# Squares of keys and queries: moved from GpSimd to VectorE, taken out of the projection's PSUM bank, and summed four tiles at a time

## The chip, the cores and the metric

The kernel runs on one core of a Trainium2 chip. The metric is the device time of one execution, in microseconds (us). The core has TensorE (PE in the rows, its weight loads PEld), VectorE (DVE), ScalarE (ACT), GpSimd (POOL) and SyncE (SP), each of which runs its own instructions in order and waits for the others by semaphores.

## The reference

One transformer block in fp32, on x of shape (2, 2048, 256): attention with 16 heads of 64, a residual and a layer norm, a gated feed-forward part with two hidden layers of 1024, another residual and layer norm. What the change touches is the RMS norm of keys and queries at the head of attention:

```python
def _rmsnorm(x, w):
    var = jnp.mean(jnp.square(x), axis=-1, keepdims=True)
    return x * jax.lax.rsqrt(var + EPS_RMS) * w

q = (x @ Wq).reshape(B, T, H, D)
k = (x @ Wk).reshape(B, T, H, D)
v = (x @ Wv).reshape(B, T, H, D)
q = _rmsnorm(q, q_rms_w)
k = _rmsnorm(k, k_rms_w)
gate_logits = jnp.einsum('bthd,hd->bht', k, u_n) / math.sqrt(D)
gate = jax.nn.softplus(gate_logits)
bias = -dist[None, None] * omega_eff[None, :, None, None] * gate[:, :, None, :]
scores = jnp.einsum('bihd,bjhd->bhij', q, k) * scale + bias
attn = jax.nn.softmax(scores, axis=-1)
y = jnp.einsum('bhij,bjhd->bihd', attn, v).reshape(B, T, H * D)
```

The mean of squares is over the 64 values of a head, for each token, head, and for q and k.

## The kernel before, in words

Three parts follow one another: attention (until about 2170 us), ffn_up and ffn_down. The change is in attention alone.

Attention works through 16 pairs of heads. One list of steps, made by `attention_steps` (line 80), sets the order on every engine: each engine walks the same list and issues what is its own, so a step's place in the list is its place in every queue. The scores of the current heads drive the list; the preparation of the next pair (projection, squares, sums, roots, norms, gate, transposes "turn", row maxima "max") is woven in at times written out by hand, in units of a head's work, t0 being the start of the pair's first head.

For pair p, 16 steps `project` (p, t), one for each 128 tokens, multiply x by the pair's weights: six matmuls of 386 columns (line 883) into one of two PSUM banks that such work takes in turn, `ps_p` and `ps_t` (`work_bank`, line 336). The 386 columns are k and q of both heads (4 x 64), two gate logits and v of both heads. ScalarE copies the bank into tile t of `raw` in SBUF (line 591) and counts up `pj_free`; `work_free` (line 339) makes TensorE wait for that count before it writes the same bank two work steps later.

GpSimd squares k and q of half the tiles (8 x 64 = 512 elements a partition) in one instruction, `square` (line 541): eight a pair, into a ring of four in `sq`. VectorE reduces each over the 64 values, `sum` (line 730): eight a pair, into `sumsq`. Then VectorE makes the inverse root by Newton steps (`root`, line 731 on; first instruction line 746), the gate (line 754 on) and the eight norms (line 766).

VectorE also has the row maxima: `max` steps, 40 a head. TensorE multiplies q by k into one of two banks `ps_m` (line 907) and VectorE takes the maximum (line 814, or 811 on the diagonal) and counts up `mx_free`; TensorE's matmul of max m waits for VectorE's max m-2:

```python
if m >= 2:
    pe.wait_ge(mx_free, m - 1)
```

TensorE's order is thus: project, max, scores, values and the rest of values of the current head, all in one queue; a wait at a max holds all that stands behind it.

Before the first pair, the VectorE step `weights` of pair 0 copies the gate's weights (line 717) and then runs `constants(4)` (line 720), a chain of constants that ends with the memset of `c_all` (line 697); the steps of pair 0 stand behind it in VectorE's queue. GpSimd's first square waits for its end (`s_const`). `sq` doubles as room for constants (`mask_f`, `pos`, `rms_in`) before the first squares.

GpSimd's main work is `e_lo`, the rest of the exponentials' split in two numbers (line 385).

Of the kernel before, what the change touches and what calls it, by code (L numbers as in the profile page):

```python
# [12 lines left out]
H, D = 16, 64  # L13
# [66 lines left out]
def attention_steps():  # L80
# [4 lines left out]
    def at(when, *step):  # L85
        extra.append((when, len(extra), step))
# [7 lines left out]
    for p in range(PAIRS):  # L94
# [5 lines left out]
        for i in range(4):  # L100
            at(t0 - 1.44 + 0.05 * i, "square", p, i)
            at(t0 - 1.38 + 0.05 * i, "sum", p, i)
            at(t0 - 1.22 + 0.04 * i, "square", p, i + 4)
            at(t0 - 1.16 + 0.04 * i, "sum", p, i + 4)
# [72 lines left out]
def attention(nc, x, wq, wk, wv, q_rms_w, k_rms_w, omega, u, yt_dram, recip_dram, rows_dram):  # L177
    ctx = ExitStack()
    with ctx:
# [20 lines left out]
        sq = sb("sq", [P, 4, HT, D])  # L200
# [38 lines left out]
        rms_in = sq[:, 1, 0:1, :]  # L239
        mask_f = sq[:, 0, 0:2, :].rearrange("p a d -> p (a d)")  # L240
        pos = sq[:, 2:4, :, :].rearrange("p i a d -> p (i a d)")
# [28 lines left out]
        pj_full = sem("pj_full")  # L270
        pj_free = sem("pj_free")
        sq_done = sem("sq_done")
# [205 lines left out]
        def _(gp):  # L478
# [42 lines left out]
            for step in steps:  # L521
# [11 lines left out]
                if step[0] == "square":  # L533
                    p, i = step[1:]
                    col, rows = (q_cols(0), q_cols(1), k_cols(0), k_cols(1))[i % 4], slice(i // 4 * HT, (i // 4 + 1) * HT)
                    gp.wait_ge(pj_free, TT * p + HT * (i // 4 + 1))
                    if p == 0 and i == 0:
                        gp.wait_ge(s_const, 1)
                    if p or i >= 4:
                        gp.wait_ge(ss_done, 8 * p + i - 3)  # L540
                    nc.gpsimd.tensor_tensor(sq[:, i % 4, :, :], raw[:, rows, col:col + D], raw[:, rows, col:col + D], ALU.mult).then_inc(sq_done, 1)
# [23 lines left out]
        def _(act):  # L565
# [6 lines left out]
            for step in steps:  # L572
# [9 lines left out]
                if step[0] == "project":  # L582
# [8 lines left out]
                    nc.scalar.activation(raw[:, t, :], work_bank(step)[:, 0:WCOLS], ACT.Copy).then_inc(pj_free, 1)  # L591
# [38 lines left out]
        def _(dve):  # L630
# [70 lines left out]
            for step in steps:  # L701
# [24 lines left out]

                if step[0] == "sum":
                    p, i = step[1:]
                    dve.wait_ge(sq_done, 8 * p + i + 1)
                    nc.vector.tensor_reduce(sumsq[:, i % 4, i // 4 * HT:(i // 4 + 1) * HT], sq[:, i % 4, :, :], AX.X, ALU.add).then_inc(ss_done, 1)  # L730
                if step[0] == "root":
                    p, i = step[1:]
                    rs, root_t, _, _ = pair_scratch(p)
                    if i == 0:
                        rooted = [ROOT * p]
                        dve.wait_ge(ss_done, 8 * (p + 1))
                        work_free(dve, step)
# [955 lines left out]
```

## Time and profile before

| | |
|---|---|
| median of 3 runs | 3400.02 us (3398.07 to 3406.59) |
| the profiled execution's own time | 3401.34 us |
| its span, from the first to the last instruction | 3399.6 us |
| mean granted TensorE clock | 0.970 |
| busy: TensorE | 3158.8 us (93%) |
| busy: ScalarE | 1794.1 us (53%) |
| busy: VectorE | 1659.2 us (49%) |
| busy: GpSimd | 1499.9 us (44%) |
| squares on GpSimd (line 541) | 128 instructions |
| sums on VectorE (line 730) | 128 instructions |

Busy time is what an engine's instructions took. Matmuls overlap, so the busy time of one is longer than its distance to the next: two starts, not a duration, tell what a matmul costs. A VectorE instruction's record also overlaps the next one's by somewhat under 0.1 us. "idle before <-releaser" names the engine, tile and line whose semaphore ended an engine's idle time. The granted clock is a share of 2.4 GHz.

### The profile page before, as it was taken

Reading aid. Unit: us, or ns where it says so; the run is one execution under the profiler, and the core shown is the slowest. Engines: PE = TensorE matmul, PEld = TensorE weight load, DVE = VectorE, ACT = ScalarE, POOL = GpSimd, SP = SyncE. Lnnn points to the kernel's source line nnn. Section 1 sums busy time; section 2 is a strip of 40 time slices with the busy share of each in tenths; the row PEclk is TensorE's granted clock in tenths of the full one; section 3 lists DMA queues with packets and bytes.
Section 4 is the critical chain, followed back from the end, with each engine's and each line's share of the span. In section 5 each row is a group of like instructions: output and inputs, shape, how many; then the busy total and the mean of one; then the engine's idle time right before and its main releaser. Section 6 shows DMA issues by size and latency. Waiting matters only on the chain. (4 is left out here: it accounts for less than half of the span.)

```text
span 3399.6 us, 45979 instructions
## 1 busy us (share of the span) xinstructions
PE 3158.8 (93%) x15472; PEld 2456.8 (72%) x15472; DVE 1659.2 (49%) x3920; ACT 1794.1 (53%) x3057; POOL 1499.9 (44%) x1318
## 2 busy tenths in 40 slices
PE   3999999999999999999999999679999999899998
PEld 3667767767767677677677677467777778688887
DVE  6565565566565665655665666142222222232322
ACT  1576676667666766766776777532222222222222
POOL 4476676566666666666766766421111110000000
PEclk6899999999999999999999999889999999899999
DMA  2242332322432422422323323432232221312120
GB/s 76 65 92 49 73 85 46 84 68 50 95 77 61 99 61 51 100 48 67 87 46 81 76 50 85 111 110 87 87 87 87 87 87 38 107 66 75 42 71 19
DMA packets 196539, 249.12 MB, mean 73 GB/s; under 512 B 67280, under 2 KB 95056, under 8 KB 196176
## 3 DMA queue, kind: packets, MB, share of 16 engines
q1 hardware_dynamic: 196304, 246.19, 28.2%
q8 instruction: 123, 2.02, 0.3%
q14 instruction: 112, 0.92, 0.1%
HBM read 84.86 MB, written 43.52 MB: 38 GB/s over the span
## 5 line engine op out<-in xcount | busy, mean ns | idle before, releaser
L385 POOL TENSOR_TENSOR e_lo<-e_all,e_hi 128x512 fp32r<-128x512 f32 (+1 forms) x832 | 1032.1, 1249 | 654.6 <-ACT e_all L627 588.8
L627 ACT ACTIVATE e_all<-ps_s,bias 128x512 f32<-128x512 f32 (+3 forms) x1280 | 788.6, 623 | 168.3 <-PE ps_s L929 80.3
L814 DVE TENSOR_REDUCE maxes<-ps_m 128x1 f32<-128x512 f32 x768 | 521.2, 686 | 371.6 <-PE ps_m L907 368.8
L620 ACT ACTIVATE e_hi<-ps_s,bias 128x512 fp32r<-128x512 f32 (+1 forms) x832 | 560.1, 673 | 228.7 <-PE ps_s L927 134.1
L907 PE MATMUL ps_m<-k_ext,q_max 128*128 128x512 f32 (+3 forms) x1280 | 462.2, 382 | 54.3 <-DVE maxes L814 25.1
L926 PE MATMUL ps_s<-q_twice,k_split 128*128 128x512 f32 (+3 forms) x1280 | 478.0, 373 | 28.3 <-ACT e_all L627 23.3
L927 PE MATMUL ps_s<-q_ext,k_ext 128*128 128x512 f32 (+3 forms) x1280 | 469.9, 367 | 0.0
L960 PE MATMUL ps_v<-e_lo,v_main 128*66 128x512 f32 (+1 forms) x832 | 431.7, 519 | 17.3 <-POOL e_lo L385 17.3
L907 PEld LDWEIGHTS ps_m<-k_ext,q_max 128*128 128x128 f32 x1280 | 245.5, 192 | 202.5 <-DVE maxes L814 59.0
L811 DVE CUSTOM_DVE_ANT_0 ps_m<-ps_m,mask_row 128x128 f32<-128x128 f32 (+3 forms) x512 | 252.5, 496 | 282.3 <-PE ps_m L907 281.9
L949 PE MATMUL ps_v<-e_hi,v_main 128*66 128x512 f32 (+1 forms) x832 | 322.2, 387 | 0.0
L944 PE MATMUL ps_v<-e_all,v_full 128*66 128x512 f32 (+2 forms) x896 | 322.2, 441 | 0.0
L951 PE MATMUL ps_v<-e_hi,v_rest 128*66 128x512 f32 (+1 forms) x832 | 320.8, 386 | 0.0
L926 PEld LDWEIGHTS ps_s<-q_twice,k_split 128*128 128x128 f32 x1280 | 242.9, 190 | 95.8 <-issue 41.0
L1162 POOL TENSOR_TENSOR y_in<-y_in,r_in 128x512 f32<-128x512 f32 x64 | 84.2, 1317 | 450.7 <-DMA r_in<-recip_sums 450.6
L927 PEld LDWEIGHTS ps_s<-q_ext,k_ext 128*128 128x128 f32 x1280 | 243.1, 190 | 31.9
L1507 POOL TENSOR_TENSOR dn_rs<-dn_rs,dn_power 128x4 f32<-128x4 f32 x8 | 8.1, 1008 | 471.8 <-DVE dn_rs L1598 471.8
L1538 ACT ACTIVATE dn_gelu<-dn_h,dn_scale 128x512 f32<-128x512 f32 x64 | 44.0, 688 | 322.8 <-PE dn_h L1637 322.8
L1225 ACT ACTIVATE gelu<-up_h,up_scale 128x512 f32<-128x512 f32 x64 | 44.1, 689 | 309.8 <-PE up_h L1382 309.8
L1637 PE MATMUL dn_h<-a_hi,h_hi 128*128 128x512 f32 x512 | 204.0, 398 | 3.7 <-DVE a_lo L1569 3.7
L960 PEld LDWEIGHTS ps_v<-e_lo,v_main 128*66 128x66 f32 x832 | 114.8, 138 | 125.7 <-issue 45.5
L1382 PE MATMUL up_h<-p_hi,h_hi 128*128 128x512 f32 x512 | 203.7, 398 | 0.0
(247 smaller groups left out, 6112.3 us busy)
## 6 DMA issues: line engine op xcount, KB each, us to landing
q_twice<-q_max SPq DMA_DIRECT2D x256, 128.0 KB, 2.3
yt<-y_out SPq DMA_DIRECT2D x128, 130.0 KB
k_ext<-kq_hi SPq DMA_DIRECT2D x128, 128.0 KB, 2.3
q_max<-kq_hi SPq DMA_DIRECT2D x128, 128.0 KB, 2.4
k_split<-kq_hi SPq DMA_DIRECT2D x128, 128.0 KB, 2.4
k_split<-kq_lo SPq DMA_DIRECT2D x128, 128.0 KB, 2.4
q_ext<-kq_lo SPq DMA_DIRECT2D x128, 128.0 KB, 2.4
y_in<-yt SPq DMA_DIRECT2D x128, 128.0 KB, 3.1
```

Source lines behind the costliest of these rows:

```text
L385: on.tensor_tensor(e_lo[:, i % LO_RING, off:QB], e_all[:, u_ % E_RING, off:QB], e_hi[:, i % HI_RING, off:QB].bitcast(F32), ALU.subtract).t ...
L620: nc.scalar.activation(e_hi[:, i % HI_RING, off:QB], ps_s[u_ % 2][:, off:QB], ACT.Exp, bias=by).then_inc(hi_done, 1)
L627: nc.scalar.activation(e_all[:, u_ % E_RING, off:QB], ps_s[u_ % 2][:, off:QB], ACT.Exp, bias=by).then_inc(ex_done, 1)
L811: nc.vector.tensor_tensor_reduce(ps_m[m % 2][:, 0:width], ps_m[m % 2][:, 0:width], mask_row[:, QB - width:QB], 1.0, NEG, ALU.add, ALU.max, ...
L814: nc.vector.tensor_reduce(maxes[:, qt, kc:kc + 1], ps_m[m % 2][:, 0:width], AX.X, ALU.max).then_inc(mx_free, 1)
L907: nc.tensor.matmul(ps_m[m % 2][:, 0:width], q_max[s][:, qt * P:(qt + 1) * P], k_ext[s][:, kc * QB:kc * QB + width], start=True, stop=True) ...
L926: nc.tensor.matmul(out, k_split[s][:, k], q_twice[grp % Q_RING][:, off:QB], start=True, stop=False)
L927: last = nc.tensor.matmul(out, k_ext[s][:, k], q_ext[s][:, q], start=False, stop=not diag)
L944: nc.tensor.matmul(bank[0:VCOLS, off:QB], v_full[s][:, kt // TQ, kt % TQ - TQ // 2, :], e_all[:, u_ % E_RING, off:QB], start=False, stop=k ...
L949: nc.tensor.matmul(bank[0:VCOLS, off:QB], v_main[s][:, kt, :], e_hi[:, i % HI_RING, off:QB], start=kt == 0, stop=False, skip_group_check=True)
L951: nc.tensor.matmul(bank[0:VCOLS, off:QB], v_rest[s][:, kt, :], e_hi[:, i % HI_RING, off:QB], start=False, stop=False, skip_group_check=Tru ...
L960: nc.tensor.matmul(ps_v[(n * NQB + qb) % 2][0:VCOLS, off:QB], v_main[s][:, kt, :], e_lo[:, i % LO_RING, off:QB], start=False, stop=kt - TQ ...
```

## The change

For each tile of the projection, VectorE now waits for ScalarE's copy (new semaphore `pj_raw`) and multiplies the 256 columns of k and q still in the PSUM bank with the copy in `raw`; the product goes to `sq`, now a ring of eight tiles of 256. Only the end of this product counts up `pj_free` and so frees the bank (and lets GpSimd take the values). After each four tiles (in the list, just behind the `project` step of the tile after them, or in the last case behind that of the last tile), one reduction over 4 x 256 elements gives the sums of four tiles. GpSimd's eight squares and VectorE's eight sums over 512 elements are gone. `sumsq` keeps its shape, its four columns now in the order of the projection's columns.

```diff
--- before.py
+++ after.py
@@ -97,11 +97,8 @@
         at(t0 - 2.05, "weights", p)
         for t in range(TT):
             at(t0 - 1.72 + 0.030 * t, "project", p, t)
-        for i in range(4):
-            at(t0 - 1.44 + 0.05 * i, "square", p, i)
-            at(t0 - 1.38 + 0.05 * i, "sum", p, i)
-            at(t0 - 1.22 + 0.04 * i, "square", p, i + 4)
-            at(t0 - 1.16 + 0.04 * i, "sum", p, i + 4)
+        for i in range(TT // TQ):
+            at(t0 - 1.72 + 0.030 * (TQ * i + 3) + 0.03, "sum", p, i)
         for i in range(ROOT_PARTS):
             at(t0 - 1.00 + 0.01 * i, "root", p, i)
         at(t0 - 0.95, "gate a", p)
@@ -197,7 +194,7 @@
         w_lo = sb("w_lo", [P, KC, WCOLS], F32R)
         wg = sb("wg", [P, KC, H])
         raw = sb("raw", [P, TT, WCOLS])
-        sq = sb("sq", [P, 4, HT, D])
+        sq = sb("sq", [P, 2 * TQ, 4 * D])
         v_main = [sb(f"v_main{i}", [P, TT, VCOLS], F32R) for i in range(2)]
         v_rest = [sb(f"v_rest{i}", [P, TT, VCOLS], F32R) for i in range(2)]
         v_full = [sb(f"v_full{i}", [P, NQB, TQ // 2, VCOLS]) for i in range(2)]
@@ -236,9 +233,9 @@
         qk_w = sb("qk_w", [P, 1])
 
 
-        rms_in = sq[:, 1, 0:1, :]
-        mask_f = sq[:, 0, 0:2, :].rearrange("p a d -> p (a d)")
-        pos = sq[:, 2:4, :, :].rearrange("p i a d -> p (i a d)")
+        mask_f = sq[:, 0, 0:P]
+        rms_in = sq[:, 1:2, 0:D]
+        pos = sq[:, TQ:2 * TQ, :].rearrange("p t c -> p (t c)")
         x_first = [raw[:].rearrange("p t c -> p (t c)")[:, (2 + 2 * i) * H * D:(4 + 2 * i) * H * D].rearrange("p (j t c) -> p j t c", t=2, c=C)
                    for i in range(2)]
         u_gate = e_all[:, 0:2, :].rearrange("p a (h d) -> p (a h) d", d=D)
@@ -268,8 +265,8 @@
         w_first = sem("w_first")
         w_done = sem("w_done")
         pj_full = sem("pj_full")
+        pj_raw = sem("pj_raw")
         pj_free = sem("pj_free")
-        sq_done = sem("sq_done")
         ss_done = sem("ss_done")
         root = sem("root")
         gate = sem("gate")
@@ -530,15 +527,6 @@
                     for k in range(KC):
                         gp.wait_ge(w_first, KC * p + k + 1)
                         nc.gpsimd.tensor_tensor(w_lo[:, k, :], w_in[:, k, :], w_hi[:, k, :].bitcast(F32), ALU.subtract).then_inc(w_done, 1)
-                if step[0] == "square":
-                    p, i = step[1:]
-                    col, rows = (q_cols(0), q_cols(1), k_cols(0), k_cols(1))[i % 4], slice(i // 4 * HT, (i // 4 + 1) * HT)
-                    gp.wait_ge(pj_free, TT * p + HT * (i // 4 + 1))
-                    if p == 0 and i == 0:
-                        gp.wait_ge(s_const, 1)
-                    if p or i >= 4:
-                        gp.wait_ge(ss_done, 8 * p + i - 3)
-                    nc.gpsimd.tensor_tensor(sq[:, i % 4, :, :], raw[:, rows, col:col + D], raw[:, rows, col:col + D], ALU.mult).then_inc(sq_done, 1)
                 if step[0] == "values in":
                     n, i = step[1:]
                     s, rows = n % 2, slice(i % 2 * HT, (i % 2 + 1) * HT)
@@ -588,7 +576,7 @@
                         act.wait_ge(gate, GATE * p)
                         act.wait_ge(normed, 8 * p)
                         act.wait_ge(v_done, 3 * 2 * p)
-                    nc.scalar.activation(raw[:, t, :], work_bank(step)[:, 0:WCOLS], ACT.Copy).then_inc(pj_free, 1)
+                    nc.scalar.activation(raw[:, t, :], work_bank(step)[:, 0:WCOLS], ACT.Copy).then_inc(pj_raw, 1)
                 if step[0] == "gate exp":
                     p = step[1]
                     act.wait_ge(gate, GATE * p + 3)
@@ -724,16 +712,21 @@
                     ins.then_inc(gate, 1)
                     dve.wait_ge(gate, gated[0])
 
+                if step[0] == "project":
+                    p, t = step[1:]
+                    dve.wait_ge(pj_raw, TT * p + t + 1)
+                    nc.vector.tensor_tensor(sq[:, t % (2 * TQ), :], work_bank(step)[:, 0:CB], raw[:, t, 0:CB], ALU.mult).then_inc(pj_free, 1)
                 if step[0] == "sum":
                     p, i = step[1:]
-                    dve.wait_ge(sq_done, 8 * p + i + 1)
-                    nc.vector.tensor_reduce(sumsq[:, i % 4, i // 4 * HT:(i // 4 + 1) * HT], sq[:, i % 4, :, :], AX.X, ALU.add).then_inc(ss_done, 1)
+                    dve.wait_ge(pj_free, TT * p + TQ * (i + 1))
+                    nc.vector.tensor_reduce(sumsq[:, :, i * TQ:(i + 1) * TQ].rearrange("p c t -> p t c"),
+                                            sq[:, i % 2 * TQ:(i % 2 + 1) * TQ, :].rearrange("p t (c d) -> p t c d", d=D), AX.X, ALU.add).then_inc(ss_done, 1)
                 if step[0] == "root":
                     p, i = step[1:]
                     rs, root_t, _, _ = pair_scratch(p)
                     if i == 0:
                         rooted = [ROOT * p]
-                        dve.wait_ge(ss_done, 8 * (p + 1))
+                        dve.wait_ge(ss_done, NQB * (p + 1))
                         work_free(dve, step)
 
                     def rlink(ins):
@@ -757,12 +750,12 @@
                     gated = [GATE * p]
                     rs, _, g, _ = pair_scratch(p)
                     for x_out in (gx[:], g[:, 0, :, :]):
-                        glink(nc.vector.tensor_tensor(x_out, logits, rs[:, 2:4, :], ALU.mult))
+                        glink(nc.vector.tensor_tensor(x_out, logits, rs[:, 0:4:2, :], ALU.mult))
                     glink(nc.vector.scalar_tensor_tensor(gs[:], gx[:], -1.0, g[:, 0, :, :], ALU.mult, ALU.min))
                 if step[0] == "norm":
                     p, i = step[1:]
                     rs = pair_scratch(p)[0]
-                    col, rows = (q_cols(0), q_cols(1), k_cols(0), k_cols(1))[i // 2], slice(i % 2 * HT, (i % 2 + 1) * HT)
+                    col, rows = i // 2 * D, slice(i % 2 * HT, (i % 2 + 1) * HT)
                     nc.vector.tensor_tensor(raw[:, rows, col:col + D], raw[:, rows, col:col + D],
                                             rs[:, i // 2, rows].unsqueeze(2).broadcast_to([P, HT, D]), ALU.mult).then_inc(normed, 1)
                 if step[0] == "gate b":
```

## Rows read from the trace of the kernel before

**Rows 1.** The page, part 1: busy us (share of the span) and instructions, TensorE.

```profile
PE 3158.8 (93%) x15472; PEld 2456.8 (72%) x15472; DVE 1659.2 (49%) x3920; ACT 1794.1 (53%) x3057; POOL 1499.9 (44%) x1318
```

**Rows 2.** Windows of pair 1: busy us (count) of PE, PEld, DVE, ACT, POOL; clock; DMA.

```profile
125.70:165.60 39.90, 39.90 (x204) 33.39 (x203) 17.81 (x43) 25.78 (x46) 20.09 (x17) 1.00 0.12 27
165.60:179.70 14.10, 14.10 (x67) 9.93 (x66) 10.56 (x23) 10.11 (x17) 11.76 (x11) 1.00 0.01 1
179.70:254.90 75.20, 69.86 (x347) 49.33 (x346) 50.48 (x132) 54.30 (x95) 53.98 (x47) 1.00 0.45 104
```

**Rows 3.** Waits of TensorE from 906 to 980 us: total us, times, longest.

```profile
PE ps_m L907 <- DVE maxes L814: 0.3, 1, 0.3
```

**Rows 4.** Timeline, the first pair, VectorE and ScalarE: start us, us, engine, line, operation.

```profile
45.48 0.09 DVE L697 MEMSET c_all<- 128x32 f32 x1
...
57.06 0.29 DVE L746 TENSOR_SCALAR mean_sq<-sumsq 128x64 f32<-128x64 f32 x1
...
45.35 0.49 ACT L591 ACTIVATE raw<-ps_t 128x386 f32<-128x386 f32 x1 [0.57 <-PE ps_t L883]
```

**Rows 5.** Groups by line and shape: count | busy us, mean ns | idle before.

```profile
L541 POOL TENSOR_TENSOR sq<-raw 128x512 f32<-128x512 f32 x128 | 132.8, 1044 | 19.7 <-DVE c_all L697 13.2 <-ACT raw L591 6.5
L730 DVE TENSOR_REDUCE sumsq<-sq 128x8 f32<-128x512 f32 x128 | 86.7, 677 | 6.0 <-POOL sq L541 6.0
...
L1585 DVE TENSOR_TENSOR dn_y<-dn_o,dn_scale_out 128x256 f32<-128x256 f32 x32 | 13.5, 423 | 20.0 <-PE dn_o L1649 20.0
...
L672 DVE TENSOR_TENSOR e_all<-e_all,sq 128x1024 f32<-128x1024 f32 x1 | 1.2, 1224 | 0.0
```

**Rows 6.** The groups by line and shape: TensorE's matmuls on e_lo, and who made them wait.

```profile
L960 PE MATMUL ps_v<-e_lo,v_main 128*66 128x512 f32 x704 | 377.5, 536 | 17.3 <-POOL e_lo L385 17.3
```

**Rows 7.** Timeline of ScalarE and VectorE, pair 7.

```profile
938.26 0.49 ACT L591 ACTIVATE raw<-ps_t 128x386 f32<-128x386 f32 x1 [0.25 <-PE ps_t L883]
946.18 0.49 ACT L591 ACTIVATE raw<-ps_p 128x386 f32<-128x386 f32 x1 [1.11 <-PE ps_p L883]
...
938.49 0.69 DVE L814 TENSOR_REDUCE maxes<-ps_m 128x1 f32<-128x512 f32 x1 [1.61 <-PE ps_m L907]
...
946.41 0.70 DVE L811 CUSTOM_DVE_ANT_0 ps_m<-ps_m,mask_row 128x512 f32<-128x512 f32 x1 [0.59 <-PE ps_m L907]
...
947.80 0.69 DVE L814 TENSOR_REDUCE maxes<-ps_m 128x1 f32<-128x512 f32 x1 [0.18 <-PE ps_m L907]
948.41 0.68 DVE L730 TENSOR_REDUCE sumsq<-sq 128x8 f32<-128x512 f32 x1
949.00 0.68 DVE L814 TENSOR_REDUCE maxes<-ps_m 128x1 f32<-128x512 f32 x1
```

**Rows 8.** Timeline of TensorE, pair 7: two maxes, and a projection tile.

```profile
940.51 0.34 PE L907 MATMUL ps_m<-k_ext,q_max 128*128 128x384 f32 x1
...
941.85 0.34 PE L883 MATMUL ps_t<-w_hi,xt_hi 128*128 128x386 f32 x1
...
949.95 0.45 PE L907 MATMUL ps_m<-k_ext,q_max 128*128 128x512 f32 x2
```

**Rows 9.** Timeline of TensorE, the first pair: first matmuls of tiles 1, 2, 11, 13.

```profile
34.63 0.53 PE L883 MATMUL ps_t<-w_hi,xt_hi 128*128 128x386 f32 x1
...
36.56 0.46 PE L883 MATMUL ps_p<-w_hi,xt_hi 128*128 128x386 f32 x1
...
44.09 0.34 PE L883 MATMUL ps_t<-w_hi,xt_hi 128*128 128x386 f32 x1
...
46.21 0.34 PE L883 MATMUL ps_t<-w_hi,xt_hi 128*128 128x386 f32 x1
```

**Rows 10.** Windows of 2 us in the first pair, with the granted clock.

```profile
34.00:36.00 2.00, 2.00 (x8) 2.00 (x7) 1.93 (x3) 0.49 (x1) 0.00 (x0) 0.50 0.00 0
...
38.00:40.00 2.00, 2.00 (x13) 2.00 (x12) 1.45 (x4) 0.92 (x2) 0.00 (x0) 1.00 0.00 0
...
54.00:56.00 2.00, 0.00 (x0) 0.00 (x0) 1.38 (x3) 0.00 (x0) 2.00 (x3) 0.50 0.00 0
```

## The prediction

> **What bounds the kernel now.** I read the page's busy times first: TensorE is busy for 93% of the span, VectorE for 49%, GpSimd for 44% [rows 1]. So work moved between VectorE and GpSimd counts only where TensorE waits for it. The second view is therefore windows over one pair. In pair 1's projection (125.7 to 165.6) TensorE is busy for 39.90 of 39.90 us, and from there to the roots for 14.10 of 14.10; only the rest of the pair has idle time, 5.3 of 75.2 us [rows 2]. All squares and sums of the pair lie in the first two windows. The waits of pair 7 say the same: between 906 and 980 us TensorE waits once, for 0.3 us, behind a max [rows 3]. In steady state there is nothing to win where the squares are; there can only be something to lose.
>
> The third view is the timeline of the first pair. Nothing of scores runs yet, and the chain of VectorE sets the pace: constants end at 45.57, the sums end just before the roots start at 57.06, and everything behind goes from there [rows 4].
>
> **GpSimd, removed.** Eight squares of 1.04 us a pair, 132.8 us in all [rows 5]. The cover is complete: in the windows that hold them TensorE never pauses [rows 2]. TensorE does wait 17.3 us in total for e_lo [rows 6], but those waits cannot be in the squares' windows, so I give this 0. If some queueing were shortened after all, 17.3 us is the most.
>
> **VectorE, removed and added.** An instruction costs its queue the distance to the next start, not its record: the sum at 948.41 is followed at 949.00, so 0.59 us for a record of 0.68 [rows 7]; I take 0.09 off each. Removed: 8 x 0.59 = 4.7 us a pair. Added squares: the nearest row is a product of 256 columns with one operand in PSUM, 423 ns [rows 5], so 0.34 us of queue; 16 make 5.4. Added sums of 1024 elements: no such reduction is in the trace. From 512 to 1024 elements a product of VectorE ends at 1224 ns [rows 5], and a reduction of 512 at 677 is alike a product's; two short sums would be 1.35. I take 1.22 (0.59 x 2 = 1.18 as the other end), 1.13 us of queue; 4 make 4.5. Net +5.2 us a pair, in a projection window where VectorE is busy for 17.8 of 39.9 us [rows 2]: room on average, so what counts is where it falls.
>
> The Trainium skill speaks against small tiles here: VectorE: DVE Perf Modes, section on the TRN2 errata, has a fixed cost per instruction, advises at least 512 elements, and gives an operation from PSUM 120 cycles plus one per element. By that a square is 0.39 us, an estimate, and the sum below would be about 1 us smaller; the row's 423 ns is used.
>
> **The bank's release, moved.** ScalarE's copy used to free the bank; now VectorE's square does. In steady state there is room: the copy that ends at 938.75 frees ps_t, whose next tile starts at 941.85 [rows 7, 8], 3.1 us later, against 0.5 for a square with its semaphores. 0 us; with a sum and a max ahead of it (1.13 + 0.60) still 2.2.
>
> **Max steps behind a square or a sum.** The square waits at the head of VectorE's queue for ScalarE's copy, and the maxes behind it wait too. TensorE wants max m's bank back at max m+2. I laid the new instructions into VectorE's order for pair 7, TensorE and ScalarE kept where they are, and compared each end with TensorE's want. Two places come late:
> - Third sum. The copy at 938.26 ends at 938.75 [rows 7]; square from 938.78, sum from 939.12, the max that ran at 938.49 now from 940.25 to 940.95. TensorE wants its bank at 940.51 [rows 8]. Late by 0.44, with 0.05 for the semaphore 0.49 us.
> - Fourth sum. The copy at 946.18 ends at 946.67; square; the max of 946.41 moves to 947.05 [rows 7]; it, the reduction and transpose behind it take until 948.19, the sum until 949.32, the maxes of 947.80 and 949.00 run at 949.32 and 949.92, the latter to 950.61. TensorE issues its two next maxes at 949.95 and, by one matmul's distance of 0.23, 950.18 [rows 8]. Late by 0.43, 0.45 with the semaphore.
> At every other max I find at least 0.28 us left. TensorE's whole queue stands behind these waits, and nothing later absorbs them: the roots behind follow TensorE's last maxes, so they slip along. 0.94 us a pair, for 15 pairs (1 to 15): 14 us. Ends: 0, if squares and sums are each a little shorter and the slack grows; 2 us a pair, 30 in all, if records do not overlap (0.09 more for each of some six instructions in a row at each place, and both waits double).
>
> **The first pair.** TensorE projects from 32.5 us, while VectorE is in its constants until 45.57 [rows 4]. Before, ScalarE freed the banks meanwhile and TensorE ran on. Now two tiles fill both banks and TensorE stands still until the squares of tiles 0 and 1, at 46.02 and 46.37. Tile 2 starts at 46.07. The granted clock was 0.50 while TensorE came from idleness and 1.00 some 4 us later, and 0.50 again once it had been idle [rows 10]; so tiles 2 and 3 cost 1.93 us each, as 34.63 to 36.56 did, and tile 4 starts at 49.93. Then a bank's round: start to the copy's end is 1.75 us (44.09 to 45.84) [rows 4, 9]; square and semaphores add 0.50; 2.25 us for two tiles where the trace has 2.12 (44.09 to 46.21) [rows 9]. Three sums on the way hold a square back by about 0.3 each. Tile 15 starts at 63.2, its copy ends at 64.96, square 65.41, last sum 66.65, roots at 66.7. Against 57.06 that is +9.6 us, whole: behind it the chain of VectorE runs without a gap and TensorE idles. Ends: 8 if the clock is full at once (2 x 0.87 less); 17 if it stays at half for the remaining tiles (11 tiles at 1.93 instead of 1.21).
>
> That ramp has a rule in the Trainium skill, TensorE: Matmul & The Clock Gate, section on the HAM clock gate: how many matmuls run at half clock after a pause varies with where the start falls. It would make this term 8 to 9.6, an estimate; the row of one start is what I sum.
>
> **Sum.** 3401.34 (the profiled execution; its span is 3399.6, the runs' median 3400.02, 1.3 lower) + 9.6 + 14 = 3425 us, +0.7%.
>
> **Rivals.**
> - *First pair alone.* The two late places have margins of half a microsecond, a hair beside a pair's 130; if they vanish, 3411. For it: VectorE is half idle. Against: the order is fixed, pairs repeat alike. 0.15.
> - *The first pair's cost is hidden*, and only the maxes' waits show: 3415. Against: TensorE has nothing at all to do at 54 to 56 us, while this chain runs [rows 10]. 0.06.
> - *VectorE becomes the bound* in the projection: all net 5.2 us a pair are exposed, 3401 + 10 + 79 = 3490; a third of it, 3437. It decides if squares or long sums take a third longer than their rows. 0.10 for anything above 3440.
> - *Faster: GpSimd's relief.* With 8.3 us a pair out of its queue, e_lo comes earlier and all 17.3 us of TensorE's waits for it go [rows 6], while the first pair hides: 3384. It decides if these waits trace back to a backlog that squares began. Against: none of them lies in the squares' windows or up to 980 us in pair 7 [rows 2, 3], and TensorE is in no wait there that could be won. 0.04.
> - *The change doesn't do what it says*: the squares still wait elsewhere, or nothing moves because banks are free anyway: 3401. 0.04.
> - The forecast: 0.61.
>
> **Numbers.** The predicted time is the forecast's, 3425. Its own ends, 8 to 17 and 0 to 30, give 3409 to 3448; both far ends at once are unlikely, and with 2 in 10 left out I say 3409 to 3442. About 0.3%, 10 us, is what a measurement can tell from no change. Slower: forecast 0.61, bound 0.10, half of the second rival and a third of the first, together 0.79. Faster 0.04. Same 0.17.
>
> **What would show it.** In the changed kernel: no row of GpSimd's sq; 256 products of 256 columns at 0.42 and 64 reductions at 1.2 us. TensorE's third tile of the first pair starts at 46, with a wait on VectorE's sq of about 9 us, and roots start at 66.7. In each later pair TensorE waits for maxes twice, 0.5 us each, near the third and fourth sum, and the distance from one pair's projection to the next grows by 0.9 us. I am wrong if that distance shrinks, if TensorE waits at a project step in steady state, or if roots of the first pair start before 60.

## The result, and the profile after

| | before | after |
|---|---|---|
| median | 3403.4 us (3398.07 to 3407.59, 6 runs) | 3432.73 us (3427.61 to 3435.67, 6 runs) |
| profiled execution, its span | 3401.34, 3399.6 us | 3433.58, 3431.8 us |
| mean granted TensorE clock | 0.970 | 0.967 |

The ratio is 1.009, with a 95% interval of 1.0077 to 1.0103: the changed kernel is 0.9% slower, some 31 us. In the two profiled executions the spans differ by 32.2 us. Of all executions below one alone was slow, one of the 11 of experiment 3 (5218.9 us, at a granted clock of 0.556), and the ratios leave it out.

The page's busy times, after:

```profile
PE 3177.9 (93%) x15472; PEld 2459.3 (72%) x15472; DVE 1739.2 (51%) x4112; ACT 1793.8 (52%) x3057; POOL 1374.0 (40%) x1190
```

Against [rows 1] VectorE has 80 us more of work and 192 more instructions, GpSimd 126 us less. Neither is near its limit. The groups by line and shape say that the new instructions are what they were meant to be, in number and in size:

```profile
L722 DVE TENSOR_REDUCE sumsq<-sq 128x16 f32<-128x1024 f32 x64 | 77.0, 1203 | 0.1
...
L718 DVE TENSOR_TENSOR sq<-ps_p,raw 128x256 f32<-128x256 f32 x128 | 54.2, 424 | 115.0 <-ACT raw L579 115.0
L718 DVE TENSOR_TENSOR sq<-ps_t,raw 128x256 f32<-128x256 f32 x128 | 54.2, 424 | 120.7 <-ACT raw L579 120.7
```

That is 256 squares at 424 ns and 64 sums at 1203 ns. The squares wait 236 us in all for ScalarE's copy at the head of VectorE's queue. That is idle time of an engine that is half idle, and costs nothing by itself.

**Where the 32 us are.** I cut the span at the start of each pair's first projection matmul and at that of its first root instruction (`mean_sq`). Pairs are numbered from 0; "the first pair" is pair 0. All in us:

| stretch | before | after | difference |
|---|---|---|---|
| to the first projection (its start) | 32.5 | 32.2 | -0.3 |
| first pair, projection to roots | 24.5 | 35.3 | +10.8 |
| first pair, roots to the next projection | 68.6 | 69.0 | +0.4 |
| pairs 1 to 15, projection to roots, each | 54.4 | 55.5 | +1.1 each, +16.5 in all |
| pairs 1 to 14, roots to the next projection, sum | 1073.9 | 1079.0 | +5.1 |
| from the roots of pair 15 to the end | 1383.8 | 1383.6 | -0.2 |

What follows the roots of pair 15 (the last heads, ffn_up, ffn_down) takes as long as before. The windows of pair 1 from projection to roots, and from there to the next projection; columns as in [rows 2]:

```profile
136.55:192.03 55.48, 55.06 (x271) 43.52 (x270) 33.85 (x80) 35.87 (x63) 23.99 (x19) 1.00 0.08 18
192.03:267.10 75.07, 69.46 (x344) 48.97 (x343) 50.04 (x132) 54.33 (x95) 54.08 (x47) 1.00 0.45 104
```

Before, TensorE never paused between projection and roots (both windows of [rows 2] are full); now it stands still for 0.42 us there. The rest of the 1.1 us is in its busy time: 55.06 us for 271 matmuls that took 54.4 before. A matmul's record is longer where it follows a wait: the one at 960.48 in pair 7 has 0.45 us, the same step had 0.34 before [rows 8]. Where TensorE waits is plainer on its weight loads. The waits on a max between projection and roots of pair 1, after and then before: total us, times, longest:

```profile
PEld ps_m L900 <- DVE maxes L807: 1.7, 4, 0.6
...
PE ps_m L900 <- DVE maxes L807: 0.3, 1, 0.3
```

```profile
PEld ps_m L907 <- DVE maxes L814: 0.3, 1, 0.3
```

And the two places in pair 7, VectorE's timeline first, then that of TensorE's weight loads:

```profile
958.27 0.42 DVE L718 TENSOR_TENSOR sq<-ps_t,raw 128x256 f32<-128x256 f32 x1 [1.28 <-ACT raw L579]
958.61 1.21 DVE L722 TENSOR_REDUCE sumsq<-sq 128x16 f32<-128x1024 f32 x1
959.74 1.28 DVE L807 TENSOR_REDUCE maxes<-ps_m 128x1 f32<-128x512 f32 x2
...
968.23 1.18 DVE L722 TENSOR_REDUCE sumsq<-sq 128x16 f32<-128x1024 f32 x1
969.32 1.96 DVE L807 TENSOR_REDUCE maxes<-ps_m 128x1 f32<-128x512 f32 x3
```

```profile
960.47 0.19 PEld L900 LDWEIGHTS ps_m<-k_ext,q_max 128*128 128x128 f32 x1 [0.64 <-DVE maxes L807]
...
970.06 0.19 PEld L900 LDWEIGHTS ps_m<-k_ext,q_max 128*128 128x128 f32 x1 [0.36 <-DVE maxes L807]
970.65 0.19 PEld L900 LDWEIGHTS ps_m<-k_ext,q_max 128*128 128x128 f32 x1 [0.41 <-DVE maxes L807]
```

The order is square, third sum, then from 959.74 the two maxes that waited behind them. TensorE's weights for the next max could have gone at 959.83 and go at 960.47. The same happens behind the fourth sum, at 970.06 and 970.65. Before, TensorE had no wait between projection and roots of this pair; the one of 0.3 us in [rows 3] lies behind the roots, which started at 960.65.

**The first pair.** TensorE's timeline, the first matmuls of tiles 2, 3 and 4, with 9.32 us of waiting before the first of them; and VectorE's, from its last constant to the roots (the square at 65.79 is that of the last tile):

```profile
45.77 0.69 PE L876 MATMUL ps_p<-w_hi,xt_hi 128*128 128x386 f32 x1 [9.32 <-DVE sq L718]
...
47.86 0.53 PE L876 MATMUL ps_t<-w_hi,xt_hi 128*128 128x386 f32 x1
...
49.80 0.52 PE L876 MATMUL ps_p<-w_hi,xt_hi 128*128 128x386 f32 x1
```

```profile
45.17 0.09 DVE L685 MEMSET c_all<- 128x32 f32 x1
45.29 0.42 DVE L718 TENSOR_TENSOR sq<-ps_p,raw 128x256 f32<-128x256 f32 x1
...
65.79 0.42 DVE L718 TENSOR_TENSOR sq<-ps_t,raw 128x256 f32<-128x256 f32 x1 [0.63 <-ACT raw L579]
66.25 1.22 DVE L722 TENSOR_REDUCE sumsq<-sq 128x16 f32<-128x1024 f32 x1
67.50 0.88 DVE L739 TENSOR_SCALAR mean_sq<-sumsq 128x64 f32<-128x64 f32 x1
```

The roots start at 67.50 instead of 57.06 [rows 4].

### The profile page after: what moved, and what is told of

Same layout as the page of the kernel before. It is cut to its first block and busy times, and to the rows that moved or that the text cites. A ratio compares the mean times of both kernels' runs of the same rounds, so it can differ in the third digit from the quotient of the medians.

```text
span 3431.8 us, 45918 instructions
## 1 busy us (share of the span) xinstructions
PE 3177.9 (93%) x15472; PEld 2459.3 (72%) x15472; DVE 1739.2 (51%) x4112; ACT 1793.8 (52%) x3057; POOL 1374.0 (40%) x1190
## 5 line engine op out<-in xcount | busy, mean ns | idle before, releaser
L900 PE MATMUL ps_m<-k_ext,q_max 128*128 128x512 f32 (+3 forms) x1280 | 470.2, 387 | 60.3 <-DVE maxes L807 30.0
L920 PEld LDWEIGHTS ps_s<-q_ext,k_ext 128*128 128x128 f32 x1280 | 243.6, 190 | 32.2
L1630 PE MATMUL dn_h<-a_hi,h_lo 128*128 128x512 f32 x512 | 203.6, 398 | 0.0
L1630 PE MATMUL dn_h<-a_lo,h_hi 128*128 128x512 f32 x512 | 203.4, 397 | 0.0
```

The source lines that it names most:

```text
L900: nc.tensor.matmul(ps_m[m % 2][:, 0:width], q_max[s][:, qt * P:(qt + 1) * P], k_ext[s][:, kc * QB:kc * QB + width], start=True, stop=True) ...
L920: last = nc.tensor.matmul(out, k_ext[s][:, k], q_ext[s][:, q], start=False, stop=not diag)
L1630: last = nc.tensor.matmul(ps_h[o % 2][:], w[:, k, col], p[:, k, :], start=k == 0 and j == 0, stop=k == OC - 1 and j == 2)
```

## The experiments

Time ratios are against the kernel before, run on the same chip between the others. Ten edited kernels ran, and both kernels once more. "Roots" is when the first pair's roots start, "pair" the distance from first projection matmul to roots in pair 7, "rest" the sum of the 14 stretches from roots to the next projection in pairs 1 to 14. The ratio comes from all executions, the other columns from the one that was profiled.

| kernel | ratio (95%) | span | roots | pair | rest |
|---|---|---|---|---|---|
| before | 1 | 3399.6 | 57.1 | 54.4 | 1073.9 |
| after | 1.0090 (1.0077 to 1.0103) | 3431.8 | 67.5 | 55.5 | 1079.0 |
| first pair frees early | 1.0060 (1.0047 to 1.0073) | 3415.9 | 55.4 | 55.5 | 1076.3 |
| late sums moved | 1.0037 (1.0024 to 1.0050) | 3409.5 | 69.1 | 54.4 | 1074.0 |
| both | 1.0006 (0.9996 to 1.0015) | 3399.7 | 55.3 | 54.4 | 1074.6 |
| fourth sum moved alone | 1.0044 (1.0031 to 1.0056) | 3411.8 | 67.8 | 55.0 | 1074.3 |
| third sum moved alone | 1.0061 (1.0044 to 1.0078) | 3414.3 | 67.8 | 54.9 | 1073.6 |
| bank freed by the copy | 1.0094 (1.0079 to 1.0110) | 3429.0 | 55.7 | 56.0 | 1081.7 |
| the same, sums moved | 1.0001 (0.9992 to 1.0010) | 3406.0 | 55.5 | 54.4 | 1077.8 |
| both, idle squares on GpSimd | 1.0001 (0.9992 to 1.0010) | 3397.5 | 55.5 | 54.4 | 1073.4 |
| both, fills on GpSimd | 0.9991 (0.9982 to 1.0000) | 3393.1 | 56.0 | 54.4 | 1070.8 |
| both, fills on ScalarE | 0.9999 (0.9988 to 1.0009) | 3395.9 | 54.2 | 54.4 | 1072.9 |
| after, once more | one execution | 3436.0 | 68.1 | 55.5 | 1079.7 |
| before, once more | one execution | 3395.8 | 56.5 | 54.4 | 1073.3 |

### 1. The first pair frees its banks early

In the first pair alone ScalarE's copy frees the bank again, and VectorE squares out of `raw`. Later pairs are as changed. The added wait keeps a square from writing over products that are not yet summed.

```diff
             if kind == "project":
-                eng.wait_ge(pj_free, TT * a + b + 1)
+                eng.wait_ge(pj_raw if a == 0 else pj_free, TT * a + b + 1)
...
-                    nc.vector.tensor_tensor(sq[:, t % (2 * TQ), :], work_bank(step)[:, 0:CB], raw[:, t, 0:CB], ALU.mult).then_inc(pj_free, 1)
+                    if t >= 2 * TQ and t % TQ == 0:
+                        dve.wait_ge(ss_done, NQB * p + t // TQ - 1)
+                    nc.vector.tensor_tensor(sq[:, t % (2 * TQ), :], raw[:, t, 0:CB] if p == 0 else work_bank(step)[:, 0:CB], raw[:, t, 0:CB], ALU.mult).then_inc(pj_free, 1)
```

> In the first pair alone ScalarE's copy frees the bank again and VectorE squares from SBUF. My theory (of the 30 us lost, 10 are the first pair's banks locked behind VectorE's constants, 16 are two late maxes a pair): TensorE projects without a pause from 32 to 52 us, VectorE runs squares and sums back to back from 45.2, 16 x 0.34 + 4 x 1.13 = 10.0 us, roots start at about 55.4 instead of 67.5; the time falls by 12 us against the changed kernel, to about 1.005 of the kernel before (3421). The distance from projection to roots in later pairs stays at 55.5 us. Rival (VectorE's added work is what costs, wherever it falls): roots still after 65 us, the time falls by under 3 us.

Measured: 3421.1 us (3415.46 to 3427.38, 5 runs) against 3401.1 (15 runs); the roots start at 55.39, 12.1 us earlier than after the change, and the distance in pair 7 stays at 55.5. The time falls by 0.30%, 10 us (the two intervals leave 4 to 16). So the first pair's cost is real, whole, and due to banks that stay locked behind VectorE's constants; the rest of the loss is elsewhere.

### 2. The late sums moved

The third and fourth sum go to later places in the list (from 1.36 and 1.24 units before t0 to 1.20 and 1.06), away from the squares and maxes that they held back.

```diff
-            at(t0 - 1.72 + 0.030 * (TQ * i + 3) + 0.03, "sum", p, i)
+            at(t0 - (1.60, 1.48, 1.20, 1.06)[i], "sum", p, i)
```

> The changed kernel with the third and fourth sum of a pair issued later in the list (t0 - 1.20 and t0 - 1.06), where the old sums stood; the work is the same. My theory: both late maxes vanish, the distance from the start of a pair's projection to its roots goes from 55.5 back to 54.4 us in each of 15 pairs, and the time falls by 16 us, to about 1.0045 of the kernel before. Rival 1 (squares, not sums, hold the maxes): the distance stays at 55.5. Rival 2 (TensorE's loss here is absorbed later in the pair): the distance falls but the time does not.

Measured: 3414.23 us (3409.66 to 3414.9, 5 runs). The distance is back at 54.4 in all of pairs 1 to 15, as TensorE's window of pair 7 shows, full from end to end:

```profile
918.35:972.78 54.43, 54.43 (x271) 43.68 (x270) 34.03 (x79) 35.88 (x63) 23.95 (x19) 1.00 0.10 22
```

VectorE does the same work there as in the changed kernel (34.0 us in 79 instructions). Nothing was taken away; two instructions stand elsewhere, and the waits are gone. This excludes VectorE's load as the bound. The time fell by some 18 us, of which the distances are 16.5. In the first pair both sums now stand behind the last tile, and its roots start 1.6 us later (69.1).

### 3. Both

> Both edits together. My theory: the gains add, 12 + 16 = 28 us less than the changed kernel, about 3404 or 1.000 to 1.001 of the kernel before; were the 5 us between roots and next projection that neither edit touches real rather than scatter of DMA waits, 1.0015. Rival (the rest of the change still costs, through VectorE's 80 us more work): over 1.003.

Edits 1 and 2 together: 3401.5 us (11 runs), ratio 1.0006. The gains add: the first pair's edit takes 0.0030 off with late sums and 0.0031 off without; the sums' edit takes 0.0053 off without the first and 0.0054 with it. The loss is these two terms, and with both gone nothing is left that could be measured, in either direction (the interval ends at 1.0015, 5 us).

### 4. The bank freed by the copy in all pairs (a miss)

As experiment 1, but in every pair: the copy frees the bank, and every square reads `raw` twice.

```diff
-                eng.wait_ge(pj_free, TT * a + b + 1)
+                eng.wait_ge(pj_raw, TT * a + b + 1)
...
-                    nc.vector.tensor_tensor(sq[:, t % (2 * TQ), :], work_bank(step)[:, 0:CB], raw[:, t, 0:CB], ALU.mult).then_inc(pj_free, 1)
+                    nc.vector.tensor_tensor(sq[:, t % (2 * TQ), :], raw[:, t, 0:CB], raw[:, t, 0:CB], ALU.mult).then_inc(pj_free, 1)
```

> In all pairs ScalarE's copy frees the bank and VectorE squares from SBUF; sums stay where the change has them. My theory: the bank's later release costs nothing in pairs 1 to 15 (3.1 us of room), so this equals the run with the first pair alone freed early, within 3 us, and TensorE still waits for two maxes a pair (55.5 us from projection to roots). Rival (the bank's release is what costs in every pair): 16 us less than that run and 54.4 us.

Measured: 3431.83 us (3429.22 to 3435.31, 4 runs), 1.0094. Some 11 us slower than experiment 1, and not the same. The distance is 56.0, longer than with the bank held. The cause is in the groups, count | busy us, mean ns of one, and in GpSimd's main work beside it:

```profile
L382 POOL TENSOR_TENSOR e_lo<-e_all,e_hi 128x512 fp32r<-128x512 f32 x704 | 905.2, 1289 | 781.1 <-ACT e_all L615 725.0 <-ACT e_hi L608 42.9 <-PE ps_v L955 6.2
...
L720 DVE TENSOR_TENSOR sq<-raw 128x256 f32<-128x256 f32 x256 | 146.7, 577 | 204.3 <-ACT raw L579 204.3
```

A square out of `raw` takes 577 ns on average where one out of the bank took 424. The timelines of VectorE, GpSimd and TensorE's weight loads in pair 7 tell when:

```profile
950.62 0.94 DVE L720 TENSOR_TENSOR sq<-raw 128x256 f32<-128x256 f32 x1 [0.71 <-ACT raw L579]
951.48 1.21 DVE L724 TENSOR_REDUCE sumsq<-sq 128x16 f32<-128x1024 f32 x1
...
953.80 0.41 DVE L720 TENSOR_TENSOR sq<-raw 128x256 f32<-128x256 f32 x1
```

```profile
949.98 1.30 POOL L382 TENSOR_TENSOR e_lo<-e_all,e_hi 128x512 fp32r<-128x512 f32 x1 [0.76 <-ACT e_hi L608]
```

```profile
953.34 0.19 PEld L902 LDWEIGHTS ps_m<-k_ext,q_max 128*128 128x128 f32 x1 [1.16 <-DVE maxes L809]
```

The square at 953.80 falls where GpSimd is idle: 0.41 us. The one at 950.62 starts inside an `e_lo` that ends at 951.28, and itself ends 0.28 us after that: 0.94 us. The whole trace repeats this: 106 squares meet no work of GpSimd and take 407 to 427 ns; 150 start inside an `e_lo`, take 414 to 999 ns, and end 0.28 to 0.38 us after its end. From the bank, the same squares kept to 411 to 427 ns beside the same `e_lo`. So PSUM as a source, which the change brought with it and the forecast gave no weight, is what kept its squares short.

The square at 950.62 is the one ahead of the third sum. It is 0.52 us longer than out of the bank; the wait of TensorE's weight loads there goes from 0.64 to 1.16 us, and the distance from 55.5 to 56.0. At the fourth sum the waits are the 0.36 and 0.41 us of the changed kernel. So this one square of a pair is what the longer distance comes from.

### 5. The fourth sum alone, and the third alone

Edit 2, but one sum at a time: (1.60, 1.48, 1.36, 1.06) is meant to leave the third where the change put it, (1.60, 1.48, 1.29, 1.24) leaves the fourth.

> The changed kernel with the fourth sum alone moved to t0 - 1.06; the third stays. A dose test. My theory (two separate late maxes): one is left, about 0.5 us, so the distance from a pair's projection to its roots is 54.9 us, half way between 54.4 and 55.5, and the time falls by half of what both moves gave, 8 to 9 us, to 1.006 to 1.0065 of the kernel before. Rival (one late place sets up the other, or a threshold): 54.4 or 55.5, all or nothing.

> The other half of the dose test: the third sum alone moved, to t0 - 1.29, the fourth stays where the change has it. My theory for the part up to the roots: one late place of about 0.5 us is left, 55.0 us from projection to roots. Beyond the roots: where the fourth sum was late, the profiles had 1076 to 1082 us in the 14 stretches from roots to the next projection, where it was not, 1074; if the late fourth sum does that, this one has 1077 or more and a ratio of 1.0055 to 1.007; if it is scatter from run to run, 1074 is as likely and the ratio is that of the run with the fourth sum moved, 1.0044.

Measured: 3415.78 us (3413.6 to 3417.65, 5 runs) and 3419.32 (3416.16 to 3424.29, 6 runs). With the fourth sum late the distance is 54.9 us in all pairs, 0.50 more than before. With the third late it is 55.0 from pair 5 on, 0.57 more. Together that is 1.07, of the 1.10 of the changed kernel: two places, each with its own wait, as forecast.

In pairs 1 to 4 of the first of these runs the distance is 54.4. There the edit did not do what was meant: 1.36 is also the time of the `project` step of tile 12, and in these four pairs the rounding of the two numbers puts the sum ahead of that step, one tile earlier than in the changed kernel. VectorE in pair 1:

```profile
168.08 1.22 DVE L722 TENSOR_REDUCE sumsq<-sq 128x16 f32<-128x1024 f32 x1
169.50 0.42 DVE L718 TENSOR_TENSOR sq<-ps_t,raw 128x256 f32<-128x256 f32 x1 [0.21 <-ACT raw L579]
```

The sum now runs in the 1.28 us in which VectorE waited for that tile's copy (the square at 958.27 above), and no max is late. So one step earlier is as good a place for the third sum as a later one.

On the whole time the fourth's move gave 0.0046 of the ratio, 16 us, and the third's 0.0029, 10 us; their distances fell by 10.2 and 9.0 us in all. With either sum moved, the rest of the pairs (1074.3 and 1073.6 in the table) is also back where it was, 5 us less. That makes 15 and 14 us, against 16 and 10 measured, which the intervals allow (6 us either way). Nor is a single profile finer than that: the stretch behind the roots of pair 15, which no edit touches, lies anywhere from 1378.1 to 1387.7 us in the fourteen profiles.

### 6. GpSimd's squares back as idle work

Experiment 3, and in 13 pairs GpSimd also does its eight old squares at their old places, into a buffer that nothing reads; before the roots VectorE waits for them. This work is added and changes no output.

```diff
+        for i in range(4 if p not in (0, 7, 8) else 0):
+            at(t0 - 1.44 + 0.05 * i, "square", p, i)
+            at(t0 - 1.22 + 0.04 * i, "square", p, i + 4)
```

> The run with both edits, plus GpSimd's eight old squares in 13 of the 16 pairs (not in pairs 0, 7 and 8), at their old places, written where nobody reads them: dead work of 104 x 1.04 = 108 us on GpSimd. My theory (taking the squares off GpSimd was worth nothing, TensorE never waited for them): the time equals the run with both edits within 2 us, 1.000 to 1.001 of the kernel before, and the distance from projection to roots stays 54.4 us. Rival (GpSimd's relief gave several us that the other terms hide): 3 us or more slower than that run.

```profile
L540 POOL TENSOR_TENSOR x_rows<-raw 128x512 f32<-128x512 f32 x104 | 108.2, 1040 | 11.3 <-DVE sq L731 9.4
```

Measured: 3400.07 us (11 runs), 1.0001 (0.9992 to 1.0010), span 3397.5, distance 54.4. With 108 us of GpSimd's work back the time doesn't rise. What the change took off GpSimd was worth nothing.

### 7. A shorter chain of constants, by GpSimd and by ScalarE

Experiment 3, with the second half of VectorE's fills (`q_max`, `q_ext` of the second buffer) given to another engine, so that VectorE's squares should start some 6 us earlier. First to GpSimd, then to ScalarE ahead of its first copy.

```diff
-                    for i in range(2):
+                    for i in range(1):
```

> The run with both edits, and the constants' fills of the second q_max and q_ext (6.2 us of VectorE in front of the first pair) moved to GpSimd, which idles there. My theory (the first pair's chain is VectorE's): GpSimd fills from 32.5 to about 44 us, VectorE's squares start at 39, and roots start when the last tile has been copied, squared and summed, at about 54 instead of 55.3; the time falls by 1.4 us against the run with both edits, to 0.999 to 1.000 of the kernel before. Rival (GpSimd takes much longer than VectorE for two-partition fills): VectorE waits for it at tile 4, roots after 56, slower than that run.

> The run with both edits, and the constants' fills of the second q_max and q_ext on ScalarE, which idles before the first copy (GpSimd's attempt slowed VectorE's own fills, 0.70 us to 1.76 a copy). Theory: ScalarE disturbs VectorE's reads of SBUF not at all, fills take 29 to 36.5 us, VectorE's fills stay at 6.2 us and end at 39.3, the squares follow the copies and roots start at 54, when the last tile is through, instead of 55.3; time 1.4 us below the run with both edits, 3 below the kernel before, at the edge of what can be measured. Rival: VectorE's fills slow down here too (SBUF's own limit), end after 42, and roots stay at 55.

On GpSimd: 3398.23 us (11 runs), 0.9991 (0.9982 to 1.0000), roots at 56.0, no earlier than without. VectorE's timeline, where half of the fills are left, first with the rest on GpSimd, then with the rest on ScalarE:

```profile
32.20 1.79 DVE L694 CAST ident_r<-ident 128x128 fp32r<-128x128 f32 x1
...
36.32 3.51 DVE L699 CAST q_max<-sq 2x1024 fp32r<-2x1024 f32 x2
...
40.58 4.67 DVE L702 CAST q_ext<-sq 2x512 fp32r<-2x512 f32 x4
45.33 0.09 DVE L703 MEMSET c_all<- 128x32 f32 x1
```

```profile
32.34 0.23 DVE L685 CAST ident_r<-ident 128x128 fp32r<-128x128 f32 x1
...
34.96 1.40 DVE L690 CAST q_max<-sq 2x1024 fp32r<-2x1024 f32 x2
...
37.12 1.77 DVE L693 CAST q_ext<-sq 2x512 fp32r<-2x512 f32 x4
38.97 0.09 DVE L694 MEMSET c_all<- 128x32 f32 x1
...
54.18 0.90 DVE L752 TENSOR_SCALAR mean_sq<-sumsq 128x64 f32<-128x64 f32 x1
```

The six copies for `q_max` and `q_ext` took 8.2 us beside GpSimd's fills and 3.2 us without. ScalarE's own fills were over at 34.62, before the first of the six, so this run does not show those copies beside ScalarE; the copy at 32.34 did run beside ScalarE's fills, and kept its 0.23 us. With ScalarE the chain ends at 39 as expected and the roots start at 54.18, 1.2 us before experiment 3's; the time is 3398.61 us (12 runs), 0.9999 (0.9988 to 1.0009), so that gain is too small to be seen. VectorE's last squares there each wait some 0.6 us for ScalarE's copy: TensorE's projection and ScalarE's copies, with the two sums behind them, and not the constants, are then what the roots wait for.

### 8. The copy frees, and the sums moved

Edits 4 and 2 together, to see whether the slow squares cost by themselves.

> Squares from SBUF in all pairs, as in the earlier run, and both sums moved. There such a square took 0.41 us alone but up to 1.0 where it overlapped an e_lo of GpSimd, against 0.42 always from the bank. Theory (two engines with two SBUF inputs each hold each other up, and only VectorE pays): still up to 1.0 us for the same tiles, GpSimd's e_lo stays 1.29; TensorE sees of it only what exceeds the room of 0.28 us and more at the maxes, so 54.4 to 54.9 us from projection to roots and 0 to 7 us more than the run with both edits. Rival (the longer squares came from the late sums' order): durations fall to 0.42.

Measured: 3403.38 us (11 runs), 1.0001 (0.9992 to 1.0010). The squares are as slow as in experiment 4 (412 to 997 ns, mean 577), the distance is 54.4. A slow square costs only where a sum and a max stand close behind it. The rest of the pair stays 4 us longer (1077.8), and nothing here says why.

### 9. Both kernels once more

> The changed kernel once more, unedited, for the scatter of the stretches that the squares don't touch. If the 5 us between roots and next projections are the change's, 1077 us or more again; if scatter, anything from 1073 on. Roots of the first pair at 67 to 68 us and 55.5 us in every pair whatever it is.

> The kernel before once more, unedited, for the same scatter: 1073 to 1075 us from roots to next projections if the kernel before is free of the extra time, up to 1079 if it is scatter. 54.4 us from projection to roots, roots of the first pair at 57.

One execution of each: 3437.78 and 3397.63 us, spans 3436.0 and 3395.8, the distances 55.5 and 54.4 again, the rest of the pairs 1079.7 and 1073.3. So the 5 us of the table of stretches repeat as a sum. Pair by pair they do not: against the kernel before, pair 10 is 2.1 us longer in the first profile of the changed kernel and 1.2 shorter in the second, pair 4 equal and then 1.8 longer. The differences arise some 25 to 45 us behind the roots, where neither squares nor sums run.

## Why the prediction was right, step by step

The forecast was 3425 us, within 3409 to 3442, by two terms, 9.6 us in the first pair and 14 us of late maxes. The median is 3432.73. Direction, places and mechanism held; each term was a little small, and one was missing. The lateness of a max is a difference of a few tenths of a microsecond between two queues, so that both came out within 0.1 us is also some luck.

- **What bounds the kernel.** TensorE's queue in steady state, VectorE's chain in the first pair: experiments 1 and 2 took each term away by itself and they add (experiment 3).
- **GpSimd's relief, given 0.** Right: experiment 6 puts 108 us of it back at no cost.
- **New instructions.** 0.42 and 1.22 us taken, 0.424 and 1.203 measured. That the square reads PSUM mattered more than the sum knew: from SBUF it would have been 0.58 (experiment 4). The estimate of 0.39 us from the Trainium skill (VectorE: DVE Perf Modes, section on the TRN2 errata) was too short; the row was nearer.
- **The bank's later release, given 0.** Right: all of TensorE's waits on a square lie in the first pair. The waits of TensorE from 40 to 70 us, and its matmuls of the projection into that bank in the whole run, are the same number:

```profile
PE ps_p L876 <- DVE sq L718: 9.6, 2, 9.3
```

```profile
L876 PE MATMUL ps_p<-w_hi,xt_hi 128*128 128x386 f32 x256 | 88.5, 346 | 21.4 <-POOL w_lo L529 11.8 <-DVE sq L718 9.6
```

- **Late maxes, 0.94 us a pair.** Mis-sized a little. The places were the two named, behind the third and the fourth sum, and no others (experiments 2 and 5). They measure 0.57 and 0.50 us, against 0.49 and 0.45. From the distances it is 1.1 us a pair and 16.5 in all, against 14. The sum took only the lateness of the max's end; what lies between that end and TensorE's matmul was reckoned 0.05 at the third place and 0.02 at the fourth.
- **The first pair, +9.6.** Measured +10.8 from start to roots (+10.4 in the start of the roots). Tile 2 started at 45.77 (46.07 forecast), tile 4 at 49.80 (49.93): two tiles at half clock were right but for a little, and the clock's windows show it, 0.50 in the first, 0.78 in the second, 1.00 in the third:

```profile
46.00:48.00 2.00, 2.00 (x7) 2.00 (x8) 0.05 (x1) 0.00 (x0) 0.00 (x0) 0.50 0.00 0
...
50.00:52.00 2.00, 2.00 (x10) 2.00 (x10) 0.42 (x1) 0.94 (x2) 0.00 (x0) 0.78 0.00 0
...
60.00:62.00 2.00, 2.00 (x12) 1.69 (x11) 1.18 (x2) 0.99 (x2) 0.00 (x0) 1.00 0.00 0
```

  From tile 4 on it came out 0.8 us longer in all: the last square started at 65.79, not 65.0, and the roots at 67.50, not 66.7. About half of that is tile 4, whose first matmuls were still at half clock: tile 5 started 1.56 us behind it, at 51.35. The rest is the rounds of two tiles, put at 2.25 us and a share of 0.3 for each sum; the four from tile 6 to tile 14 took 2.57 each.
- **Roots to the next projection, given nothing.** The step that is missing: +5.1 us. The sum assumed that what comes late just slips along. Its cause is open.
- **The rivals.** First pair alone: excluded by experiment 2. First pair hidden: excluded by experiment 1. VectorE as the bound: excluded by experiment 2, the same load at no wait. Faster by GpSimd's relief: excluded by experiment 6.

**What stays open.** The 5 us between roots and projection. The profiles with both sums late have 1079.0, 1079.7 and, with the first pair freed early, 1076.3; those with squares out of SBUF in all pairs 1081.7 and 1077.8; all nine others 1070.8 to 1074.6. The groups do not overlap, but single pairs scatter by 2 us either way and each kernel has one or two profiles. That a late VectorE shifts a transfer or GpSimd's work against TensorE's order would fit, and was not tried by itself.

No kernel tried is measurably faster than the one before: those with both terms removed are at 0.9991 to 1.0006, and the lowest of these (experiment 7, on GpSimd) has an interval that touches 1.

## What to carry to other kernels

An engine that is half idle is still not free at every place: ask of each new instruction in its queue who waits for the one behind it, and lay it out against the times at which the bottleneck wants its buffers back. Here two sums at the wrong place cost 16 us and at another place none; for the third, one step in the list was enough, because VectorE was idle just before. And a buffer's release is best given to the engine that is on time from the very first tile; a chain of constants ahead of it turns into idle time of TensorE, once, at the start.

## What the runs showed of the hardware

- **VectorE and GpSimd hold each other up, and the one that starts first keeps its time.** Experiment 4 has 150 squares with both operands in SBUF that start inside an `e_lo`: up to 1.00 us instead of 0.41, ending 0.28 to 0.38 us after the `e_lo`, which keeps its 1289 ns. None of its squares starts first, so it shows one order only. The feed-forward part of the changed kernel shows the other, VectorE's timeline and then GpSimd's:

```profile
2628.69 0.69 DVE L1296 TENSOR_TENSOR p_lo<-prod,p_hi 128x512 fp32r<-128x512 f32 x1 [0.70 <-ACT p_hi L1207]
```

```profile
2628.70 1.83 POOL L1155 TENSOR_TENSOR y_in<-y_in,r_in 128x512 f32<-128x512 f32 x1 [32.15 <-DMA r_in<-recip_sums]
2630.72 1.29 POOL L1155 TENSOR_TENSOR y_in<-y_in,r_in 128x512 f32<-128x512 f32 x1 [0.19 <-DMA r_in<-recip_sums]
```

  VectorE's product, first by 0.01 us, keeps its 0.69; GpSimd's takes 1.83 us where the next takes 1.29, and ends 1.15 us after VectorE's. With one operand in PSUM all squares of the changed kernel stayed at 411 to 427 ns beside the same `e_lo`. Copies with a single SBUF operand suffered too (experiment 7: 3.51 and 4.67 us for 1.40 and 1.77, and 1.79 for 0.23 beside a memset of GpSimd). The Trainium skill, GPSIMD Engine Reference, section Specifications, says that the two engines share SBUF interfaces and contend where VectorE's instruction has two SBUF inputs or runs in a 2-port mode; the trace agrees.
- **A long reduction is barely cheaper than two short ones.** 1024 elements 1203 ns, 512 elements 677 ns [rows 5]: 11% less than two of the short ones for the same work, and 4% by the distance to the next start (1.13 us against twice 0.59).
- **Two partitions cost GpSimd as much as all 128.** Its `tensor_tensor` on 2x512 takes 1.10 us, on 128x512 1.04 [rows 5]; on 2x1024 it takes 1.89 (the records below join several, some 0.08 us apart). Each on 2x512 began in the last 0.2 us of a copy of VectorE, so a little waiting may be in it. Its `tensor_scalar` on 2x1024 took 3.5 us, but beside VectorE's copies, so how much of that is its own is not shown. VectorE's copy of 2x1024, undisturbed, takes 0.69. Experiment 7, GpSimd's timeline:

```profile
33.98 3.85 POOL L544 TENSOR_TENSOR q_max<-sq,one 2x1024 fp32r<-2x1024 f32 x2
37.92 3.52 POOL L545 TENSOR_SCALAR q_max<-sq 2x1024 fp32r<-2x1024 f32 x1
41.52 4.63 POOL L547 TENSOR_TENSOR q_ext<-sq,one 2x512 fp32r<-2x512 f32 x4
```
